# Where an opened matmul group is closed: at the end of a filler step, or at the start of the next one

## The chip, the cores and the metric

The kernel runs on all 8 cores of one Trainium2 chip. Each core works alone on its share: one of four batches and one half (8 heads, 512 columns) of the 1024 features. No data passes between cores. The metric is device time in microseconds (us) of the slowest core.

## The reference

With x of shape (4, 4096, 1024):

```python
xn = layernorm(x)
q, k, v = split(xn @ qkv_weights)          # 16 heads of 64, causal softmax attention
s  = softmax(mask(q @ k / 8)) @ v
xq = clip(round(xn / x_scale), -128, 127)  # x_scale = max|xn| / 127 per row
g  = silu((xq @ weight_q.T) * x_scale * weight_scale + bias)
out = x + s * g
```

(k is reshaped without the usual transpose, which is why the kernel scatters it in an unusual order; this doesn't matter here.)

## The kernel before

One Python program, `build_program`, appends instructions to five lists, one per engine, in the order in which its helpers are called. Every engine then replays its list strictly in that order. So the order of calls in the program is the order of work on each engine, and a wait of one instruction holds up all that stand behind it on the same engine.

**Phase 1** (up to about 600 us) walks over the 32 row tiles of x. For each it normalises, transposes and projects k (`emit_tile_a1`), and in between it pours in the steps that make v, the gate g and q of the first four chunks of 512 rows (`pump_merged`). The diff leaves this phase alone.

**Phase 2** is attention, by chunks c = 0 to 7 of 512 query rows (`emit_attention_chunk`). A chunk has four head pairs P, and each pair 4c+4 key blocks jb. One (P, jb) is a *unit*. In a unit the program emits, in this order: a piece of the gating of the pair before, if one is due (`pend_gate`, one of ga1, ga2, gb1, gb2, at jb 0, 2, 3 and 4, ahead of which it calls `close_open()`); the two matmuls Oa and Ob of the unit three back (L794, L798); the two score matmuls into sT (L735, L741; in the diagonal blocks L748 to L773); the exp on ScalarE (L780); and then a call of `pump()`. sT has two buffers and eT three.

`pump()` is the filler. Phase 2 still has to prepare the chunks 4 to 7, and `pump()` spreads that work over the units, usually one step of it per unit (`budget` is 1 in all units here that have steps left). The steps of a chunk stand in two lists: `flatA` (28 small steps of layernorm, quantisation and transposes, one that ends them, then v, then the gate), and `ib["lst"]` (q), which is taken up as soon as the 29th step of `flatA` is done.

The steps that matter here are the matmul groups, 12 per chunk: four q groups (`emit_qkv_f`, L538), four v groups (`emit_v_sub`, L555) and four gate groups (`emit_ffn_oc`, L585). Each group is 8 matmuls of 512 columns that accumulate in the one PSUM tile `pm`. It is cut into two steps of 4 matmuls each. The first half carries the tag "open": `pm` is then half summed, and nothing else may write it until the second half has run. The second half also emits what empties `pm`: ScalarE copies it to qT (L544) for q, VectorE copies it to v_aug (L562) for v, and VectorE multiplies it into g1s (L590) for the gate. The gate then has a chain of its own: t_b on GpSimd (L594), tanh on ScalarE (L600), gT on VectorE (L605), and the next g1s stands behind that gT in VectorE's list. The first matmul of any group waits until `pm` has been emptied of the group before it (`dep["pm_free"]`). `pm` has other users too: the single-row product of `emit_ffn_pre` (L569) and the eight tiny matmuls of ga2 (L848, L852).

`drain_open()` runs the second half wherever the last step taken was an open one. Before the change, `pump()` calls it after its step, so both halves of a group are emitted one behind the other.

Of the 52 groups in phase 2, four (q of chunk 3) are emitted in attention chunk 1, and 12 each in the attention chunks 2 to 5. The place of each is (pump number within the chunk, and the gating piece that stands at the start of that unit, if any):

- chunk 1: q at 1 (ga1), 2, 3 (ga2), 4 (gb1)
- chunk 2: q at 30 to 33; v at 35, 36, 37 (ga1), 38; gate at 41 (gb2), 42, 43, 44
- chunk 3: q at 30, 31, 32, 33 (ga1); v at 35 (ga2), 36 (gb1), 37 (gb2), 38; gate at 41 to 44
- chunk 4: q at 30 to 33; v at 35 to 38; gate at 41 (ga1), 42, 43 (ga2), 44 (gb1)
- chunk 5: q at 30 to 33; v at 35 to 38; gate at 41 to 44

The pumps 34 and 39 of a chunk carry steps without any instruction, pump 40 carries `emit_ffn_pre`. In chunk 2 pump 39 has ga2 ahead of it.

Of the kernel before, what the change touches and what calls it, by code (L numbers as in the profile page):

```python
# [67 lines left out]
def build_program(S=4096):  # L68
# [600 lines left out]
    def a_substeps(tc):  # L669
# [31 lines left out]
        return steps, stepsB  # L701

    def emit_attention_chunk(c, pump, close_open, drain_pre, drain_full):
        for P in range(NPAIR):
            if P == 1:
                drain_full()
# [10 lines left out]
            for jb in range(njb):  # L717
                if P == 0 and jb == 4 * c - 1:
                    drain_pre()
# [85 lines left out]
                pend_av.append(mk_av())  # L805
                att["unit"] += 1
                pump()
            while pend_av:
                pend_av.pop(0)()
# [154 lines left out]
    def append_tc(tc):  # L964
        sa, sb = a_substeps(tc)
        sa = norm(sa)
        for j, (fn, tag) in enumerate(sa):
            if tag and tag.startswith("tilesdone"):
                qa_tiles_end[tc] = len(flatA) + j + 1
                sa[j] = (fn, None)  # L970
            elif tag and tag.startswith("vdone"):
                qa_pre_end[tc] = len(flatA) + j + 1
                sa[j] = (fn, None)
        flatA.extend(sa)
        qa_end[tc] = len(flatA)
        qb[tc] = norm(sb)
# [25 lines left out]
    def stepA():  # L1002
        fn, tag = flatA[ia["k"]]
        fn()
        ia["k"] += 1
        return tag

    def stepB():
        fn, tag = ib["lst"][ib["k"]]
        fn()  # L1010
        ib["k"] += 1
        return tag

    def drain_open():
        while (ia["k"] > 0 and ia["k"] < len(flatA)
               and flatA[ia["k"] - 1][1] == "open"):
            stepA()
        while (ib["k"] > 0 and ib["k"] < len(ib["lst"])
               and ib["lst"][ib["k"] - 1][1] == "open"):
            stepB()  # L1020

    for c in range(NTC):
        def drain_pre(c=c):
            while ia["k"] < qa_pre_end.get(c, qa_end.get(c, 0)):
                stepA()

        def drain_full(c=c):
            while ia["k"] < qa_end.get(c, 0):
                stepA()
        while ia["k"] < qa_start.get(c, 0):  # L1030
            stepA()
        if c == 0:
            drain_pre()
        while ib["k"] < len(ib["lst"]):
            stepB()
        if NMERGE <= c + 2 < NTC:
            append_tc(c + 2)
        ib["lst"] = qb.get(c + 2, [])
        ib["k"] = 0
        ib["gate"] = qa_tiles_end.get(c + 2, 0)  # L1040

        uc = {"u": 0}
        nunits = NPAIR * (4 * c + 4)
        dlA = 0

        def pump():
            uc["u"] += 1
            left = max(1, nunits - uc["u"] + 1)
            needed = max(0, dlA - ia["k"]) + (len(ib["lst"]) - ib["k"] + 1) // 2
            budget = max(1, -(-needed // left))  # L1050
            for _ in range(budget):
                if ib["k"] < len(ib["lst"]) and ia["k"] >= ib["gate"]:
                    stepB()
                elif ia["k"] < len(flatA):
                    stepA()
                else:
                    break
            drain_open()

        def close_open():  # L1060
            drain_open()
        emit_attention_chunk(c, pump, close_open, drain_pre, drain_full)
    while ia["k"] < len(flatA):
        stepA()
# [36 lines left out]
def _get_nc(S):  # L1101
    if S not in _NC_CACHE:
        _NC_CACHE[S] = build_program(S)
    return _NC_CACHE[S]
# [44 lines left out]
```

How the kernel before makes its waits and increments, by code:

```python
    def replay(self, eng, handle, sems):  # L47
        seen = {}
        own = self.OWN.get(eng)
        prior = 0
        for waits, fn, inc in self.ops[eng]:
            allw = list(waits)
            if own is not None and prior > 0:
                allw.append((own, prior))
            for s, v in allw:
                if seen.get(s, 0) >= v:
                    continue
                handle.wait_ge(sems[s], v)
                seen[s] = v
            ins = fn(handle)
            if inc is not None:
                s, amt = inc
                ins.then_inc(sems[s], amt)
                if s == own:
                    prior += amt
```

## Time and profile before

| | us |
|---|---|
| median of the runs | 1527.43 (1524.6 to 1530.26) |
| the profiled execution | 1525.28 |
| its slowest core's span (core 4) | 1523.7 |
| spans of all eight cores | 1503.6 to 1523.7 |
| matmuls busy (PE), core 4 | 1067.1 |
| ScalarE busy (ACT), core 4 | 720.1 |
| VectorE busy (DVE), core 4 | 575.8 |

In the rows further down, PE is TensorE with its matmuls, ACT is ScalarE, DVE is VectorE and POOL is GpSimd. A row of the timeline gives the start and the length in us, the engine, the line, what is written from what, and how many instructions are merged into the row; in brackets stands the idle time of the engine before it and whose end released it. A matmul's listed length holds the pipe's tail, so the pace of back-to-back matmuls is read from start to start. PEclk is the share of full TensorE clock that was granted in a stretch: 1.00 is 2.4 GHz and 0.50 would be 1.2 GHz throughout.

### The profile page before, as it was taken

The page shows a single profiled execution, that of the slowest core. Times are in us where ns is not written, and L with a number is a line of the kernel's source. Part 1 is how long each engine was busy: PE and PEld are TensorE (multiplying, and loading weights), DVE is VectorE, ACT ScalarE, POOL GpSimd, SP SyncE. Part 2 cuts the span into 40 slices and gives each one's busy share as a digit, 9 for nine tenths or more (in the row PEclk, how much of TensorE's full clock was granted, in tenths as well). Part 3 has the DMA queues.
Part 4 walks back from the last instruction along what each step waited for, and adds up shares of the span by engine and source line. Part 5 has one row for each costly group of instructions (what it writes and reads, how often), then busy time and mean ns, then how long its engine had stood idle before and what let it go on. Part 6 is the DMA issues. An engine that isn't in the chain of part 4 may idle for free.

```text
span 1523.7 us, 17831 instructions; the slowest of 8 cores (1503.6 to 1523.7 us)
## 1 busy us (share of the span) xinstructions
PE 1067.1 (70%) x5163; PEld 435.6 (29%) x5200; DVE 575.8 (38%) x1086; ACT 720.1 (47%) x905; POOL 302.1 (20%) x412
## 2 busy tenths in 40 slices
PE   0235545545455556987888888888888888888886
PEld 0112221212222122543333333433333333323232
DVE  0385283483553554337437335431822111111111
ACT  0121131220211112475445456548646888888886
POOL 1341250430513543113122013011301000000000
PEclk9956856758666655698887998989888999899999
DMA  7110010000000121112111002001100000000000
GB/s 115 49 42 14 14 42 0 28 29 0 29 27 28 56 70 49 42 42 70 43 29 56 15 15 84 8 8 42 36 8 21 14 15 14 15 28 9 11 17 14
DMA packets 24463, 47.46 MB, mean 31 GB/s; under 512 B 4272, under 2 KB 7472, under 8 KB 24368
## 3 DMA queue, kind: packets, MB, share of 16 engines
q1 hardware_dynamic: 15552, 25.34, 5.7%
q0 software_dynamic: 8816, 20.98, 5.6%
q8 instruction: 44, 0.72, 0.2%
q14 instruction: 51, 0.42, 0.1%
HBM read 40.54 MB, written 8.39 MB: 32 GB/s over the span
## 4 chain that ended last, share of the span: by engine, by line
PE 35%; DVE 25%; ACT 18%; issue 9%; POOL 6%; DMA 6%; DVEq 1%; ACTq 0%; POOLq 0%; SPq 0%
ACT eT L780 16%; PE Oa L794 5%; PE pm L555 4%; PE pm L538 4%; PE Ob L798 4%; DMA xst<-x 3%; PE pm L585 3%; PE sT L735 3%; DVE t_r L433 3%; DVE t_b L437 3%; DMA w8n<-w 2%; DVE bnst L240 2%; PE pm L848 2%; DVE t_g L430 2%; PE pm L852 2%
## 5 line engine op out<-in xcount | busy, mean ns | idle before, releaser
L780 ACT ACTIVATE eT<-sT 128x1024 bf16<-128x1024 f32 (+1 forms) x576 | 549.5, 954 | 214.4 <-PE sT L741 121.4
L794 PE MATMUL Oa<-eT,v_aug 128*65 128x512 bf16 (+1 forms) x576 | 238.5, 415 | 2.8
L798 PE MATMUL Ob<-eT,v_aug 128*65 128x512 bf16 (+1 forms) x576 | 226.3, 397 | 0.0
L735 PE MATMUL sT<-qT,kTa 64*128 64x512 bf16 x448 | 182.2, 416 | 36.2 <-ACT eT L780 34.5
L741 PE MATMUL sT<-qT,kTa 64*128 64x512 bf16 x448 | 185.0, 422 | 0.0
L897 POOL DMA_DIRECT2D out<-outs x32 | 24.3, 760 | 687.5 <-DVE outs L890 602.4
L833 DVE TENSOR_TENSOR wpr<-Oa,gT 64x512 bf16<-64x512 f32 x32 | 21.8, 683 | 336.8 <-PE Ob L798 335.8
L301 PE MATMUL sT<-Wqk,xnK 128*128 128x512 bf16 x244 | 107.2, 614 | 51.2 <-ACT xnK L289 40.1
L735 PEld LDWEIGHTS sT<-qT,kTa 64*128 64x128 bf16 x448 | 40.3, 94 | 222.6 <-issue 219.9
L794 PEld LDWEIGHTS Oa<-eT,v_aug 128*65 128x65 bf16 x576 | 67.2, 117 | 106.0 <-issue 94.1
L585 PE MATMUL pm<-xnq,wqT 128*128 128x512 bf16 x251 | 75.0, 451 | 26.4 <-DVE g1s L590 20.4
L555 PE MATMUL pm<-Wv,xnq 128*128 128x512 bf16 x247 | 70.0, 430 | 24.4 <-DVE v_aug L562 18.8
L281 PE MATMUL pt<-idb_s,xnbf 128*128 128x128 bf16 x128 | 17.2, 280 | 95.8 <-POOL xqbf L269 83.1
L594 POOL TENSOR_SCALAR t_b<-g1s,wscb,biab 128x512 f32<-128x512 f32 x32 | 24.6, 769 | 296.1 <-DVE g1s L590 296.1
L289 ACT ACTIVATE xnK<-pt 128x1024 bf16<-128x1024 bf16 x32 | 32.8, 1025 | 98.8 <-PE pt L281 92.4
L305 ACT ACTIVATE ktmp<-sT 128x512 bf16<-128x512 f32 x32 | 19.1, 598 | 123.8 <-PE sT L301 123.8
L240 DVE BATCH_NORM_STATS2 bnst<-xst 128x6 f32<-128x512 f32 x64 | 44.4, 694 | 87.5 <-DMA xst<-x 82.0
L848 PE MATMUL pm<-idf_s,rows 1*128 1x1 f32 x256 | 50.5, 264 | 33.1 <-DVE wpr L837 21.8
L538 PE MATMUL pm<-xnq,Wqk 128*128 128x512 bf16 x246 | 60.8, 387 | 17.8 <-ACT qT L544 8.7
L798 PEld LDWEIGHTS Ob<-eT,v_aug 128*65 128x65 bf16 x576 | 69.5, 121 | 7.0 <-issue 0.5
L600 ACT ACTIVATE g1s<-t_b 128x512 f32<-128x512 f32 x32 | 20.2, 631 | 96.5 <-POOL t_b L594 96.5
L562 DVE CAST v_aug<-pm 128x512 bf16<-128x512 f32 x32 | 22.2, 694 | 113.4 <-PE pm L555 113.2
(122 smaller groups left out, 1603.1 us busy)
## 6 DMA issues: line engine op xcount, KB each, us to landing
xst<-x SPq DMA_DIRECT2D x96, 256.0 KB, 2.9
xres<-xr POOLq DMA_DIRECT2D x32, 256.0 KB, 3.7
out<-outs POOLq DMA_DIRECT2D x32, 256.0 KB, 2.8
Wqk<-wq POOLq DMA_DIRECT2D x1, 1024.0 KB, 14.8
Wqk<-wk POOLq DMA_DIRECT2D x1, 1024.0 KB, 25.8
Wv<-wv POOLq DMA_DIRECT2D x1, 1024.0 KB, 30.4
w8n<-w POOLq DMA_DIRECT2D x4, 256.0 KB, 2.7
wscb<-wsc SPq DMA_DIRECT2D x4, 0.5 KB, 6.7
```

The costliest lines, as they stand in the source:

```text
L240: sc.emit("vector", lambda v, buf=buf, h2=h2, bnst=bnst: v.bn_stats(bnst[:, 6 * h2:6 * h2 + 6], xst[:, 512 * buf:512 * buf + 512]), waits= ...
L301: c_mm = sc.emit("tensor", lambda t, kk=kk, xK=xK, slotA=slotA: t.matmul(slotA, xK[:, kk, :], Wqk[:, kk, 512:1024], start=(kk == 0), stop= ...
L433: v.scalar_tensor_tensor(t_r[:], txn[:, off:off + 512], inv, t_g[:], ALU.mult, ALU.subtract), inc="dv")
L538: c_mm = sc.emit("tensor", lambda t, kk=kk, f=f: t.matmul(pm[:], Wqk[:, kk, 128 * f:128 * f + 128], xnq[:, kk, :], start=(kk == 0), stop=( ...
L555: c_mm = sc.emit("tensor", lambda t, kk=kk, vs=vs: t.matmul(pm[:], xnq[:, kk, 128 * vs:128 * vs + 128], Wv[:, kk, :], start=(kk == 0), sto ...
L585: c_mm = sc.emit("tensor", lambda t, kk=kk, oc=oc: t.matmul(pm[:], wqT[:, kk, 128 * oc:128 * oc + 128], xnq[:, 8 + kk, :], start=(kk == 0) ...
L735: t.matmul(sT[par][:, o:o + w], kTa[0:64, P, 128 * jb:128 * jb + 128], qT[P][0:64, qb + o:qb + o + w], start=True, stop=True), waits=w0)
L741: qb=qb: t.matmul(sT[par][:, 512 + o:512 + o + w], kTa[64:128, P, 128 * jb:128 * jb + 128], qT[P][64:128, qb + o:qb + o + w], start=True, ...
L780: s.activation(eT[pe3][:].rearrange("p (b n) -> p b n", b=2)[:, :, o:o + w], sT[par][:].rearrange("p (b n) -> p b n", b=2)[:, :, o:o + w], ...
L794: sc.emit("tensor", lambda t: t.matmul(Oa[:, o:o + w], v_aug[:, jb, 65 * hA:65 * hA + 65], eT[pe3][:, o:o + w], start=(jb == 0), stop=(jb ...
L798: c_av = sc.emit("tensor", lambda t: t.matmul(Ob[:, o:o + w], v_aug[:, jb, 65 * hB:65 * hB + 65], eT[pe3][:, 512 + o:512 + o + w], start=( ...
L848: c_lt = sc.emit("tensor", lambda t, it=it: t.matmul(pm[0:128, 2 * it:2 * it + 1], rows[64:65, 128 * it:128 * it + 128], idf[64:65, 64:65] ...
```

## The change

`pump()` calls `drain_open()` ahead of its budget of steps and no longer behind it. A group whose first half was emitted in one unit gets its second half at the next call of `pump()`, or at the next `close_open()` if a gating piece comes first. In between stand the Oa, Ob and score matmuls of the next unit. So that no step of another list, and no other user of `pm`, comes between the halves, `drain_open()` is also called at the start of `drain_pre`, of `drain_full` and of each chunk.

```diff
     for c in range(NTC):
         def drain_pre(c=c):
+            drain_open()
             while ia["k"] < qa_pre_end.get(c, qa_end.get(c, 0)):
                 stepA()
 
         def drain_full(c=c):
+            drain_open()
             while ia["k"] < qa_end.get(c, 0):
                 stepA()
+        drain_open()
         while ia["k"] < qa_start.get(c, 0):
             stepA()
...
             budget = max(1, -(-needed // left))
+            drain_open()
             for _ in range(budget):
                 if ib["k"] < len(ib["lst"]) and ia["k"] >= ib["gate"]:
                     stepB()
@@
                     stepA()
                 else:
                     break
-            drain_open()
```

No instruction is added, removed or changed in shape; only the places of some instructions in the engines' lists change.

## Rows read from the trace of the kernel before

**Rows 1.** The page, part 1: engine, busy us, share, instructions.

```profile
PE 1067.1 (70%) x5163; PEld 435.6 (29%) x5200; DVE 575.8 (38%) x1086; ACT 720.1 (47%) x905; POOL 302.1 (20%) x412
```

**Rows 2.** Timeline, units without filler in chunk 6, ScalarE, then TensorE.

```profile
1174.00 8.84 ACT L780 ACTIVATE eT<-sT 128x1024 bf16<-128x1024 f32 x8
...
1173.21 0.39 PE L735 MATMUL sT<-qT,kTa 64*128 64x512 bf16 x1
...
1174.08 0.39 PE L735 MATMUL sT<-qT,kTa 64*128 64x512 bf16 x1
```

**Rows 3.** Timeline, v groups of chunk 5, TensorE, with the unit between two groups.

```profile
1127.48 0.39 PE L735 MATMUL sT<-qT,kTa 64*128 64x512 bf16 x1
1127.48 0.39 PE L741 MATMUL sT<-qT,kTa 64*128 64x512 bf16 x1
1128.03 1.67 PE L555 MATMUL pm<-Wv,xnq 128*128 128x512 bf16 x7 [0.16 <-issue]
1129.54 0.38 PE L794 MATMUL Oa<-eT,v_aug 128*65 128x512 bf16 x1
1129.75 0.38 PE L798 MATMUL Ob<-eT,v_aug 128*65 128x512 bf16 x1
1130.07 0.39 PE L735 MATMUL sT<-qT,kTa 64*128 64x512 bf16 x1
1130.07 0.39 PE L741 MATMUL sT<-qT,kTa 64*128 64x512 bf16 x1
1130.71 1.89 PE L555 MATMUL pm<-Wv,xnq 128*128 128x512 bf16 x8 [0.26 <-DVE v_aug L562]
1132.44 0.38 PE L794 MATMUL Oa<-eT,v_aug 128*65 128x512 bf16 x1
...
1133.62 1.89 PE L555 MATMUL pm<-Wv,xnq 128*128 128x512 bf16 x8 [0.26 <-DVE v_aug L562]
```

**Rows 4.** Timeline, the same stretch, VectorE.

```profile
1129.88 0.69 DVE L562 CAST v_aug<-pm 128x512 bf16<-128x512 f32 x1 [14.23 <-PE pm L555]
```

**Rows 5.** Timeline, phase 1, TensorE: groups with nothing between them.

```profile
247.51 1.89 PE L555 MATMUL pm<-Wv,xnq 128*128 128x512 bf16 x8 [1.01 <-DVE v_aug L562]
250.42 1.89 PE L555 MATMUL pm<-Wv,xnq 128*128 128x512 bf16 x8 [1.01 <-DVE v_aug L562]
...
262.79 3.57 PE L585 MATMUL pm<-xnq,wqT 128*128 128x512 bf16 x8 [1.01 <-DVE g1s L590]
267.38 3.57 PE L585 MATMUL pm<-xnq,wqT 128*128 128x512 bf16 x8 [1.01 <-DVE g1s L590]
...
281.03 1.89 PE L538 MATMUL pm<-xnq,Wqk 128*128 128x512 bf16 x8 [0.90 <-ACT qT L544]
283.81 1.89 PE L538 MATMUL pm<-xnq,Wqk 128*128 128x512 bf16 x8 [0.90 <-ACT qT L544]
```

**Rows 6.** Timeline, q groups of chunk 5, TensorE, then ScalarE.

```profile
1118.57 1.89 PE L538 MATMUL pm<-xnq,Wqk 128*128 128x512 bf16 x8
...
1120.83 0.39 PE L735 MATMUL sT<-qT,kTa 64*128 64x512 bf16 x1
...
1121.46 1.89 PE L538 MATMUL pm<-xnq,Wqk 128*128 128x512 bf16 x8 [0.25 <-PE sT L741]
...
1124.35 1.89 PE L538 MATMUL pm<-xnq,Wqk 128*128 128x512 bf16 x8 [0.25 <-PE sT L741]
...
1120.61 0.60 ACT L544 ACTIVATE qT<-pm 128x512 bf16<-128x512 f32 x1 [1.00 <-PE pm L538]
1121.37 1.03 ACT L780 ACTIVATE eT<-sT 128x1024 bf16<-128x1024 f32 x1 [0.16 <-PE sT L741]
```

**Rows 7.** Timeline, gate groups, TensorE: four of chunk 5, two of chunk 4.

```profile
1142.51 1.67 PE L585 MATMUL pm<-xnq,wqT 128*128 128x512 bf16 x7 [0.55 <-ACT xscBs L574]
...
1145.19 1.89 PE L585 MATMUL pm<-xnq,wqT 128*128 128x512 bf16 x8 [0.26 <-DVE g1s L590]
...
1148.64 1.89 PE L585 MATMUL pm<-xnq,wqT 128*128 128x512 bf16 x8 [0.81 <-DVE g1s L590]
...
1152.15 1.89 PE L585 MATMUL pm<-xnq,wqT 128*128 128x512 bf16 x8 [0.87 <-DVE g1s L590]
...
1003.57 1.90 PE L585 MATMUL pm<-xnq,wqT 128*128 128x512 bf16 x8
1006.49 1.89 PE L585 MATMUL pm<-xnq,wqT 128*128 128x512 bf16 x8 [0.69 <-DVE g1s L590]
```

**Rows 8.** Busy time by stretch, with PEclk: phase 1 (three rows), then phase 2.

```profile
247.50:256.40 8.90, 5.79 (x24) 2.33 (x26) 2.08 (x3) 0.00 (x0) 0.00 (x0) 1.00 0.00 0
275.40:286.60 11.20, 7.49 (x31) 2.85 (x32) 2.77 (x4) 3.02 (x5) 1.47 (x2) 1.00 0.00 0
262.70:271.90 9.20, 7.15 (x16) 2.04 (x16) 2.77 (x4) 1.26 (x2) 1.54 (x2) 0.55 0.00 0
1128.00:1139.00 11.00, 10.19 (x47) 4.00 (x46) 2.50 (x4) 4.28 (x5) 0.00 (x0) 1.00 0.01 1
```

## The prediction

> **What bounds the kernel now.** I read the page first for the engines' loads, then the timeline engine by engine inside phase 2, since an average over the span can't say which engine sets the pace where the filler runs. By the page [rows 1] no engine is full; the answer lies in two kinds of stretch.
>
> In units without filler, ScalarE runs its exps without a break: eight in 8.84 us, 1.10 us each [rows 2]. TensorE alone, while it runs ahead of ScalarE's backlog, needs 0.87 us from one score matmul to the next (1174.08 - 1173.21). There ScalarE is the bound, by 0.23 us a unit. In units with a matmul group TensorE adds 8 matmuls, and ScalarE idles (its exp of 1.03 us and a copy of 0.60 us fit in a unit of 2.9 us with over a microsecond left) [rows 6]. There the TensorE list sets the pace, and what is lost on it is lost for the whole core: the next scores, and so the next exp, come that much later, and nothing later gives it back, because ScalarE then has no backlog.
>
> The row on which all hangs is the wait for `pm`. A v group starts 1130.71, the next 1133.62: 2.90 us apart [rows 3], of which the 8 matmuls take 1.73 (from its first to the start of Oa, 1130.71 to 1132.44) and the attention unit 0.87; the rest, about 0.3, is a wait for VectorE's copy. Now compare phase 1, where groups follow each other with nothing between: v groups again start 2.90 us apart (247.51, 250.42), with 1.01 us listed as idle before each [rows 5]. The two distances are equal. So emptying `pm` makes a fixed distance of 2.90 us between two v groups, and the attention unit costs nothing there: it runs inside the wait. The pieces of that wait: the last matmul of a group starts at about 1129.33 (0.21 before Oa), the copy starts at 1129.88 and takes 0.69 [rows 4], and the next group starts 0.14 after its end. From the last matmul's start to the next group's first: 0.55 + 0.69 + 0.14 = 1.38 us, where a matmul that doesn't wait would follow after 0.22. The wait is worth 1.16 us.
>
> **The change part by part.** No work is added. Between two scores of a series there are still 8 filler matmuls, but they are now the second half of group X and the first half of group Y, next to each other. The wait for the emptying of `pm` lies exactly between those two. The list on TensorE was: X first, X second, Oa, Ob, scores, Y. It becomes: X second, wait, Y first, Oa, Ob, scores, Y second. The attention unit that covered the wait now stands between the two halves of one group, where nothing waits. Behind the waiting first matmul of Y stand Oa, Ob and the next scores, and for those waits ScalarE.
>
> How many such places are there? Two groups in pumps that follow each other, with no gating piece at the start of the second's unit: with a gating piece, `close_open()` runs the second half of X ahead of it, the order on TensorE stays X, gating, unit, Y, and nothing changes. From the list of places: q has 1, 3, 2, 3 and 3 in the chunks 1 to 5, that is 12; v has 2, 1, 3 and 3 in the chunks 2 to 5, that is 9; the gate has 3, 3, 1 and 3, that is 10. Together 31 of 52 groups.
>
> *v, 9 places.* The distance becomes the bare one plus the unit that no longer hides: 2.90 + 0.87 = 3.77 against 2.90, +0.87 each [rows 2, 3, 5]. 9 x 0.87 = 7.8 us.
>
> *q, 12 places.* Bare distance 2.78 (281.03 to 283.81) [rows 5], now 2.89 [rows 6]. Lower bound 2.78 + 0.87 - 2.89 = +0.76. But the copy to qT now stands behind the exp of its unit in ScalarE's list. The exp starts 0.54 after its score matmul (1121.37 - 1120.83) and takes 1.03 [rows 6], so it ends 1.57 after it; the copy's 0.60 with 0.05 before it ends at 2.22; 0.14 later, at 2.36, the next first half starts; its four matmuls take 0.86 and Oa, Ob up to the next score matmul 0.53 (1129.54 to 1130.07) [rows 3]: a distance of 3.75, +0.86. An upper bound takes the 0.25 that TensorE stood still there before a group, now seen after a score matmul [rows 6], in place of 0.14: +0.97. I take the middle one, since both its ends are rows: 12 x 0.86 = 10.3 us (9.1 to 11.6).
>
> *Gate, 10 places.* Here the chain g1s, t_b, tanh, gT, g1s already holds the groups 3.45 to 3.51 us apart from the third on, and only the first distance is short, 2.68 [rows 7]. The new distance: from the start of g1s 0.69, 0.14 to the next first half, 0.86 for it, 0.87 for the unit, 0.65 from the first to the last matmul start of the second half, 0.55 to its g1s: 3.76. That is above 3.5, so the chain no longer decides and is hidden. A series of four: 3 x 3.76 - (2.68 + 3.45 + 3.51) = +1.6. Three series 4.9, the single place in chunk 4 (2.92 now) +0.8: 5.7 us. If the chain's slack counted fully against it, the lower bound would be 0.25 a place, 2.5 us.
>
> *The ends of the series.* The second half of the last v group moves into the unit after it, and `emit_ffn_pre` in the next finds `pm` not yet empty: its place comes 0.31 + 0.86 + 0.53 + 0.31 = 2.01 after the score matmul, `pm` is free at 0.31 + 0.65 + 1.38 = 2.34, +0.33 in three chunks (in chunk 2 ga2 lies there): +1.0. From q to v the same sum is 2.36 against 2.01, and 0.24 of it is lost there already (1127.48 to 1128.03, where 0.31 would do) [rows 3]: +0.1 each, +0.4. At the end of the four gate series half a group moves into a unit in which ScalarE's pace of 1.10 would have ruled over TensorE's 0.87 [rows 2]: -0.23 each, -0.9. Net +0.5.
>
> *The other edits.* The calls of `drain_open()` in `drain_pre`, `drain_full` and at the chunk's start find nothing open: the first two come where their loops have no step to run, and each series ended before the chunk did. Free. No DMA is moved: the steps that issue x loads (SP) or GpSimd work other than t_b are not open ones and stay in their unit. t_b moves with its group, and GpSimd is 20% busy [rows 1].
>
> Sum: 7.8 + 10.3 + 5.7 + 0.5 = 24.3 us on the profiled execution's 1525.3, which gives 1549.6. The median of the runs is 2.1 higher, so 1551.7; I say 1552. What isn't in the sum is the clock.
>
> **The rivals.**
>
> *A. The wait is there and the clock falls too.* A unit of 3.76 us has 8 filler matmuls and four of attention in it, TensorE streaming for 2.60 (1.73 + 0.87), 69%, where it was 90%. Against a fall: in phase 1, groups 2.90 and 2.78 us apart stream 60 to 62% of the time, and the clock stayed at 1.00 (2.4 GHz) [rows 8]. For it: gate groups in phase 1, 4.59 us apart, ran at a granted 0.55, close to 1.2 GHz, with 3.57 us a group in place of 1.89 [rows 5, 8], after a stretch of single-row products. A clock that is low when a series begins could stay low through it. Each unit at the low clock would add 3.57 - 1.89 = 1.68 for the group and about as much again in proportion, 0.7, for the attention matmuls: 2.4 us. If a third of the 31 units ran so: +25, 1577. If all did: +74, 1626.
> The Trainium skill, TensorE: Matmul & The Clock Gate, section "A second HAM failure mode: psum-queue depth-cycling", says that frequent small idles between matmul groups, caused by turning over PSUM, make the clock swing between its two levels. By that rule rival A would be the forecast. The trace only half agrees: two stretches with a 0.9 to 1.0 us idle before every group kept 1.00, the third didn't [rows 8].
>
> *B. The wait is covered after all.* If VectorE and ScalarE emptied `pm` fast enough, only the odd us would move, and the time would be 1525 to 1532. The 1.01 us idle before every back-to-back v group and the 0.90 before every q group in phase 1 speak against it [rows 5]: there both engines had nothing else to do and it was still paid.
>
> *C. Faster.* This would be the smoothing of load: half groups in a unit leave less TensorE time between two exps. Where a half group stood alone in a unit, the unit would take 1.73 and let ScalarE catch up. It decides only if TensorE's per-unit work falls below ScalarE's 1.10, and with a half group it is 1.73. Only the ends of the series gain, 0.23 each [rows 2]; even if all 13 series gave 0.23 and no wait appeared: -3, 1524. For over 2% it would need the clock: if phase 2 as a whole got a better clock through other timing, up to the 20 us by which the cores of one execution differ, 1507.
>
> **How the numbers follow.** Forecast 0.70, A 0.20, B 0.07, C 0.03. The likeliest: 1552, its own range 1544 (the lower bounds of q and gate: 24.3 - 1.2 - 3.2 = 20, less 3 for timing) to 1562 (q's upper bound and three or four units more at the low clock). The range over the cases that hold 8 in 10 is 1541 to 1576: below it lie B and C, above it the heavier half of A. A measurement of this kernel can tell about 2% (30 us) from no change. The forecast and the light end of A stay below 1558, the line for 2% slower; A mostly and the upper end of the forecast pass it. Faster 0.02, same 0.70, slower 0.28.
>
> **What would show it right or wrong.** In the timeline of chunk 5 after: rows of four matmuls at L555, a wait of about 1.0 us put down to v_aug L562, four more, Oa, Ob, scores; v groups 3.77 apart, q groups 3.75, gate groups 3.76. In the waits: idle before L538, L555 and L585 for `pm` up by about 25 us in all, busy times unchanged, PEclk in these series still 1.00. Everything after chunk 5 lies about 24 us later and is otherwise unchanged. Wrong would be: PEclk near 0.5 in the series (A); the same distances with no idle (B); or distances as I say but a span that grows by much less, which would mean that the lost time is given back in a place where I hold ScalarE to have no backlog.

## The result, and the profile after

The changed kernel takes 1551.6 us (median; before, in the same comparison, 1525.48). The ratio is 1.0161, with a 95% interval of 1.013 to 1.0192: slower by 25 us, which is clear of the noise and less than 2%. The forecast was 1552, from a median of 1527.4 before; in this comparison that median was 1525.5.

The waits of TensorE in the stretch where filler runs (600 to 1190 us of the changed kernel, core 4): who waited for whom, us in total, times, longest. First the three that the change makes:

```profile
PE pm L538 <- ACT qT L544: 14.8, 13, 2.0
PE pm L585 <- DVE g1s L590: 10.8, 11, 1.0
PE pm L555 <- DVE v_aug L562: 10.0, 10, 1.2
```

The same view of before, 600 to 1160 us:

```profile
PE pm L585 <- DVE g1s L590: 6.5, 10, 0.9
PE pm L555 <- DVE v_aug L562: 3.2, 7, 1.3
...
PE pm L538 <- ACT qT L544: 0.7, 1, 0.7
```

35.6 us in place of 10.4: 25 us more idle in front of groups. The busy times are as before (PE 1070.8 against 1067.1, ACT 718.7 against 720.1). The timeline of TensorE in chunk 5 after, v groups (start, length, engine, line, out<-in, count, idle before and its releaser):

```profile
1158.88 1.04 PE L555 MATMUL pm<-Wv,xnq 128*128 128x512 bf16 x4
1160.94 1.02 PE L555 MATMUL pm<-Wv,xnq 128*128 128x512 bf16 x4 [1.02 <-DVE v_aug L562]
1161.80 0.38 PE L794 MATMUL Oa<-eT,v_aug 128*65 128x512 bf16 x1
1162.01 0.38 PE L798 MATMUL Ob<-eT,v_aug 128*65 128x512 bf16 x1
1162.32 0.39 PE L735 MATMUL sT<-qT,kTa 64*128 64x512 bf16 x1
1162.33 0.39 PE L741 MATMUL sT<-qT,kTa 64*128 64x512 bf16 x1
1162.65 1.04 PE L555 MATMUL pm<-Wv,xnq 128*128 128x512 bf16 x4
```

The reader should see the four matmuls of one group's second half, a wait of 1.02 us, four of the next group's first half, and only then the attention unit. In [rows 3] the unit stood between the groups and 0.26 us of wait was left. The distance is 3.77 us (1162.65 - 1158.88).

The q groups of the same chunk, TensorE and then ScalarE; they answer to [rows 6]:

```profile
1143.21 0.39 PE L735 MATMUL sT<-qT,kTa 64*128 64x512 bf16 x1
...
1143.54 1.04 PE L538 MATMUL pm<-xnq,Wqk 128*128 128x512 bf16 x4
1145.73 1.02 PE L538 MATMUL pm<-xnq,Wqk 128*128 128x512 bf16 x4 [1.16 <-ACT qT L544]
...
1147.44 1.04 PE L538 MATMUL pm<-xnq,Wqk 128*128 128x512 bf16 x4
...
1143.76 1.02 ACT L780 ACTIVATE eT<-sT 128x1024 bf16<-128x1024 f32 x1 [2.08 <-PE sT L741]
1144.88 0.60 ACT L544 ACTIVATE qT<-pm 128x512 bf16<-128x512 f32 x1
```

The copy stands behind the exp. It ends at 1145.48, and TensorE goes on 0.25 later. The distance is 3.90.

The gate groups of chunk 5, which answer to [rows 7], 3.76 apart:

```profile
1172.15 1.04 PE L585 MATMUL pm<-xnq,wqT 128*128 128x512 bf16 x4
1174.20 1.02 PE L585 MATMUL pm<-xnq,wqT 128*128 128x512 bf16 x4 [1.01 <-DVE g1s L590]
...
1175.91 1.04 PE L585 MATMUL pm<-xnq,wqT 128*128 128x512 bf16 x4
```

Busy time by stretch for the three series, the columns as in [rows 8]; the last but two is the granted clock:

```profile
1138.00:1153.00 15.00, 11.40 (x51) 3.98 (x50) 0.00 (x0) 6.97 (x9) 0.30 (x1) 1.00 0.06 18
1154.00:1167.00 13.00, 9.96 (x46) 3.47 (x44) 2.08 (x3) 3.82 (x5) 0.00 (x0) 1.00 0.00 0
1171.00:1180.00 9.00, 6.97 (x33) 2.42 (x31) 2.24 (x4) 4.01 (x6) 1.53 (x2) 1.00 0.01 2
```

TensorE stays at 2.4 GHz through all three. Not every series runs at that level: in four of the 13 (q of chunk 1, v of chunks 2 and 3, the gate of chunk 4), and for part of the gate of chunk 2, the granted clock is partly 0.50, in both kernels. Summed over the 13 series, the time at 1.2 GHz is 17.6 us before and 17.5 after (mean of the eight cores, worked out from the granted clock between the exps at the ends of each series). So the clock has no part in the 25 us.

Where the time went by chunk, from one profiled execution of each kernel: the start of a chunk's first exp to that of the next chunk's, mean of the eight cores, after less before.

| | phase 1 | c0 | c1 | c2 | c3 | c4 | c5 | c6 | c7 |
|---|---|---|---|---|---|---|---|---|---|
| before, us | 593.0 | 33.9 | 56.4 | 109.2 | 127.0 | 140.7 | 155.3 | 136.0 | 164.0 |
| after less before | +1.9 | +0.4 | +2.3 | +5.6 | +4.7 | +5.5 | +6.7 | -0.8 | -1.3 |
| adjacent places | 0 | 0 | 1 | 8 | 6 | 7 | 9 | 0 | 0 |

The loss lies in the chunks that have adjacent groups. Phase 1 is the same code in both kernels, so its +1.9 shows by how much two executions differ anyway.

### The profile page after: what moved, and what is told of

Its sections match the earlier page's. It is cut to its first block, busy times and chain, and to the rows that moved or that the text cites. A ratio compares the mean times of both kernels' runs of the same rounds, so it can differ in the third digit from the quotient of the medians.

```text
span 1550.9 us, 17819 instructions; the slowest of 8 cores (1526.8 to 1550.9 us)
## 1 busy us (share of the span) xinstructions
PE 1070.8 (69%) x5161; PEld 435.1 (28%) x5200; DVE 575.8 (37%) x1086; ACT 718.7 (46%) x905; POOL 302.1 (19%) x412
## 4 chain that ended last, share of the span: by engine, by line
PE 36%; DVE 25%; ACT 18%; issue 9%; POOL 6%; DMA 5%; DVEq 1%; ACTq 0%; POOLq 0%; SPq 0%
ACT eT L780 16%; PE Oa L794 5%; PE pm L555 4%; PE pm L585 4%; PE Ob L798 4%; PE pm L538 3%; PE sT L735 3%; DVE t_r L433 3%; DVE t_b L437 3%; DMA xst<-x 3%; DMA w8n<-w 2%; PE pm L848 2%; DVE t_g L430 2%; PE pm L852 2%; DVE bnst L240 2%
## 5 line engine op out<-in xcount | busy, mean ns | idle before, releaser
L741 PE MATMUL sT<-qT,kTa 64*128 64x512 bf16 x448 | 183.3, 418 | 0.0
L897 POOL DMA_DIRECT2D out<-outs x32 | 24.3, 758 | 695.7 <-DVE outs L890 613.3
L555 PE MATMUL pm<-Wv,xnq 128*128 128x512 bf16 x247 | 72.6, 433 | 33.3 <-DVE v_aug L562 27.1
L562 DVE CAST v_aug<-pm 128x512 bf16<-128x512 f32 x32 | 22.2, 694 | 134.1 <-PE pm L555 133.9
```

What stands on the lines that cost most here:

```text
L555: c_mm = sc.emit("tensor", lambda t, kk=kk, vs=vs: t.matmul(pm[:], xnq[:, kk, 128 * vs:128 * vs + 128], Wv[:, kk, :], start=(kk == 0), sto ...
L741: qb=qb: t.matmul(sT[par][:, 512 + o:512 + o + w], kTa[64:128, P, 128 * jb:128 * jb + 128], qT[P][64:128, qb + o:qb + o + w], start=True, ...
```

## The experiments

The theory: a lost microsecond wherever the second half of one group and the first half of the next stand next to each other on TensorE, because emptying `pm` then lies bare. The rivals: that every split group costs something (1.61% over 52 groups), that the clock is lower, and that the order costs something through ScalarE.

**One kind of group at a time, and only where no other group follows.** The changed kernel, in which `pump()` still closes a group in its own unit unless a condition holds:

```diff
+            if not (ib["k"] > 0 and ib["k"] <= len(ib["lst"]) and ib["lst"][ib["k"] - 1][1] == "open"):
+                drain_open()
```

This is `q_only`: the condition says that the last step taken from the q list was an open half. It is written likewise for v, for the gate, and for the 21 groups behind which no other group stands in the next unit or a gating piece comes first (`free_only`).

> Only the q groups are left open over a unit; v and gate groups are closed in their own pump, as before. Adjacency theory (cost only where the second half of one group and the first half of the next stand next to each other, with the emptying of pm between them): 12 such places, each the distance after of 3.90 less 2.89 before = 1.0 us, and 0.3 at each of the four steps from q to v: +13 us, ratio 1.008 to 1.009. Split theory (every opened half costs the same, 25 us over 52 groups = 0.48): 20 q groups, +10 us at most, and it must agree with the cost per group of the other three runs. Clock theory (the loss is a lower TensorE clock in the series): PEclk under 1.00 in the q series, cost not tied to places.

> Only the v groups are left open over a unit. Adjacency theory: 9 places of 0.87 us and 0.33 at three steps to the single-row product: +9 us, ratio 1.006. Split theory: 16 groups, +7.7 us. Clock theory: no fixed relation to places.

> Only the gate groups are left open over a unit. Adjacency theory: the chain over GpSimd and ScalarE already held these groups 3.5 us apart, so 10 places give only +5.7, less 0.9 at the ends: +5 us, ratio 1.003. Split theory: 16 groups, +7.7 us. If the waits for pm simply added up without the chain's cover, 10 x 0.87 = +8.7.

> Groups are left open only where no other group follows in the next unit, or where a gating piece closes them first; the 31 adjacent places are closed in their own pump as before. Adjacency theory: 21 opened groups, none adjacent, only the ends of series move: within 2 us of before, ratio 1.000 +- 0.002. Split theory: 21 x 0.48 = +10 us, ratio 1.007.

| split groups | of them adjacent | ratio to before | 95% interval |
|---|---|---|---|
| 20 q | 12 | 1.0134 | 1.0101 to 1.0168 |
| 16 v | 9 | 1.0073 | 1.0045 to 1.0101 |
| 16 gate | 10 | 1.0026 | 1.0001 to 1.0051 |
| 21, none adjacent | 0 | 0.9996 | 0.9972 to 1.0019 |

The last row is the cleanest, but it holds fewer split groups than its label says. In nine of the 21, `close_open()` brings the second half right behind the first on TensorE; in the trace of `free_only` 12 groups really have other matmuls between their halves (in two of them only the last Oa and Ob of a pair, a case that the prediction took for no change), and in the changed kernel 31 + 12 = 43. By that count the split theory asks for 25/43 x 12 = 7 us, +0.5%. The interval ends at +0.2%: tearing a group apart costs nothing that could be measured, as long as no other group touches it. In the first row the waits of v and gate stay those of before, and that of q is the one of after:

```profile
PE pm L538 <- ACT qT L544: 14.7, 13, 1.9
PE pm L585 <- DVE g1s L590: 6.8, 11, 0.9
PE pm L555 <- DVE v_aug L562: 3.5, 8, 1.3
```

v came out near what was expected (+11 us against +9) and so did the gate (+4 against +5). q missed: +20 us against +13, with an interval that begins above the 1.008 to 1.009 expected. The three add up to 2.3%, more than the 1.6% of all together; with the widths of the intervals the two may just meet. The q series of chunk 3 explains a part: in the profiled execution it took 4.7 us more than before at only two adjacent places, with 3.1 us more at the low clock. Why the clock was low there stays open.

**Half a group per unit.** One bank; a pump that closes a group opens none:

```diff
+            k0 = ia["k"] + ib["k"]
             drain_open()
+            if ia["k"] + ib["k"] > k0:
+                budget -= 1
```

> One bank; a pump that closes a group takes no further step, so a unit holds one half group at most and each group takes two units. Adjacency theory: between the second half of a group and the first half of the next stands a whole unit, so no wait is paid that is not covered. Also units of 1.73 us in place of one of 2.60 + 0.3 and one without filler of 1.10, in which ScalarE is the bound: for 36 q and v groups 3.46 against 3.99 = -0.5 each, for 16 gate groups 3.5 against 4.6 = -1.1 each at most: -15 to -35 us, ratio 0.977 to 0.990. Rival (ScalarE's backlog makes smoothing worthless, only waits count): 21 x 0.3 and the gate's waits, -12 us at most, ratio 0.992. Split theory: slower than the changed kernel.

1.0048 (1.0017 to 1.0080): a miss of my own theory, which had asked for 0.977 to 0.990. The split theory missed as well (the run was faster than the changed kernel), and so did the rival that only waits count (0.992). By chunk, against before, it was -6.5, +17.1, -7.0 and +2.9 us in c2 to c5. So the series gain and something takes it back. Core 3 in chunk 3, TensorE and then ScalarE:

```profile
895.55 2.94 PE L585 MATMUL pm<-xnq,wqT 128*128 128x512 bf16 x8 [1.68 <-ACT xscBs L574]
899.50 0.55 PE L848 MATMUL pm<-idf_s,rows 1*128 1x1 f32 x2 [1.01 <-DVE g1s L590]
...
903.57 3.31 PE L585 MATMUL pm<-xnq,wqT 128*128 128x512 bf16 x8
...
895.50 1.02 ACT L780 ACTIVATE eT<-sT 128x1024 bf16<-128x1024 f32 x1
900.50 0.63 ACT L600 ACTIVATE g1s<-t_b 128x512 f32<-128x512 f32 x1 [3.98 <-POOL t_b L594]
903.74 1.02 ACT L780 ACTIVATE eT<-sT 128x1024 bf16<-128x1024 f32 x1 [2.60 <-PE sT L741]
```

The longer series now runs into units with gating pieces. There `close_open()` pushes the second half in front of the piece, and ga2, which uses `pm` too, waits for g1s. A whole group, the wait, and eight single-row products at the low clock stand between two scores: 8.2 us from one exp to the next. The mean of the eight cores for this unit is 7.6 us; before, when it held no group, it took 2.5.

**Two banks.** The groups use `pm` and the bank of `pt` in turn. This was run with the order of after (`two_banks`), with that of before (`two_banks_b`) and with half a group per unit (`half_two_banks`). Of the edit only the choice of the bank is shown:

```diff
+        if half == 0 and bk["on"]:
+            if bk["key"] == "pm_free":
+                bk["t"], bk["key"] = pt[:].bitcast(F32), "pt_free"
+            else:
+                bk["t"], bk["key"] = pm[:], "pm_free"
```

> The changed kernel's order, but in phase 2 the groups accumulate in turn in pm and in the bank of pt (read as 512 f32), so a group waits for the emptying of the group two before it. Adjacency theory (the wait for the single bank is the whole cost): the 1.0 us waits before q and v groups vanish, v and q distances fall to about 2.6 us, the gate stays at 3.5 by its own chain: 24 to 30 us less than the changed kernel, and 3 to 7 us less than before: ratio to before 0.995 to 0.998. Rival (the order itself costs, through ScalarE's late exps or the weights): it stays near 1.016.

> The same two banks with the order of before (both halves of a group together). Adjacency theory: before, the attention unit covers 0.87 of the 1.16 us wait and 0.3 is left; without it 21 v and q places save 0.3 each, and the gate nothing: 6 us less than before, ratio 0.996, and equal to the run with the changed order within 3 us.

> One half group per unit, and two banks. Adjacency theory: with a unit between groups nothing waits for a bank, so the second bank brings nothing more: the same as one half per unit with one bank, within 3 us.

1.0047 (1.0016 to 1.0077), 1.0031 (1.0009 to 1.0053) and 0.9960 (0.9939 to 0.9981). With the second bank the changed order costs 0.2% more than the old one, where with one bank it cost 1.6%. The waits of the groups for the copies to qT and v_aug and for g1s are gone from the list of waits. That shows the wait for the single bank to be nearly the whole difference between the two orders. The expectations of the times failed in all three runs, though. Neither order became faster than before. A part of the reason comes out below: a group that starts right behind gb2 waits for the bank of `pt`. `two_banks_b` has two such groups that land there, the gate group at pump 41 of chunk 2 and the v group at pump 37 of chunk 3; with the unit behind it, each place took 2.8 and 3.3 us longer than before (mean of the eight cores). That is 6 of the 11 us between the +5 measured and the -6 expected; the rest stays open. And half a group per unit did gain from the second bank, 0.9% or 13 us, where I had written that nothing waits. The unit between two groups covers only 0.87 of the 1.16 us, as [rows 3] had shown already; 0.3 us in each of some 36 distances makes an estimated 10 us of it.

**Half a group per unit, away from the gating pieces.** From chunk 2 on, no group is opened in a unit whose next one is among a pair's first five (jb 0 to 4, where the gating pieces stand), nor a gate group in a pair's last three units; what is left over slips into the next chunk. Of the edit only the rule is shown:

```diff
+                    if tag == "open" and (nx < 5 or (      # nx: jb of the next unit
+                            gate_step and nx > 4 * c + 4 - 3)):
+                        break
```

> The same with the single bank pm. A unit covers 0.87 of the 1.16 us wait, so 0.3 is left in each of some 36 distances between groups: 10 us more than with two banks, ratio 0.987 to 0.994. If the bank doesn't matter once the halves stand alone, it equals the run with two banks.

> One half group per unit, two banks, and no group is opened in a unit whose next unit begins with a gating piece (nor a gate group in the last three units of a pair), so no half is pushed together with a gating piece; the steps left over slip into the next chunk. Collision theory (one half per unit loses its gain where its series meets the gating pieces: +18 us and +15 us behind the series of chunks 3 and 5): those losses vanish and what the series gain stays, 0.5 us for a q or v group and up to 1.1 for a gate group, 8 us a chunk in four chunks: -20 to -30 us against before, ratio 0.980 to 0.987. Rival (the loss belongs to spreading itself, that is, to a lower clock and ScalarE's backlog in longer series): ratio 0.996 as without the rule, or worse, since the series are still longer.

> The same with two banks, but chunk 2, which has only 48 units for 57 steps, keeps the order of before (whole groups), so nothing slips out of it. Collision theory: -8 us in each of the chunks 3 to 5 and nothing in chunk 2: -15 to -25 us, ratio 0.984 to 0.990. If it beats the run with the rule in all chunks, chunk 2 is too short for spreading.

With one bank: 0.9901 (0.9868 to 0.9934), 1506.1 us, faster than both kernels and within what was expected of it. The rule does two things at once, though: it keeps the groups away from the gating pieces, and it moves steps into the units of later chunks. No run separates the two. That half a group per unit lost its gain to the collisions is therefore argued from the rows above, not shown by itself. With two banks the rule gained nothing, where 0.980 to 0.987 had been expected: 1.0008 (0.9988 to 1.0029), and with chunk 2 left in the old order 1.0013 (0.9996 to 1.0029, expected 0.984 to 0.990). The timeline of the first of these two says why. TensorE in chunk 4, core 5, then VectorE:

```profile
916.44 0.60 PE L754 MATMUL sT<-qT,kTa 64*128 64x512 bf16 x1
919.11 1.86 PE L567 MATMUL pt<-Wv,xnq 128*128 128x512 bf16 x4 [2.06 <-DVE outs L903]
...
915.97 0.28 DVE L897 SCALAR_TENSOR_TENSOR outs<-pt,linvT,xres 128x64 f32<-128x64 bf16 x1 [2.55 <-PE pt L889]
...
918.68 0.28 DVE L903 SCALAR_TENSOR_TENSOR outs<-pt,linvT,xres 128x64 f32<-128x64 bf16 x1
```

(This kernel has more lines: L567 is the v group, L555 elsewhere, and L754, L897 and L903 are L741, L884 and L890.) The bank of `pt` isn't free. gb2 has just put its transposes there, and VectorE reads them in eight steps over 3 us; the rule lets a group start right behind gb2, and it landed in `pt`. Six such units stand in the chunks 3 to 5; they took 5.3 to 5.7 us each, and 1.8 to 2.6 in the run with one bank (mean of the eight cores). The last run changes that one thing: a group always takes `pm` if the next unit is among a pair's first seven. By the rule those are the groups that start in the unit of gb2 and in the one behind it.

```diff
-            if bk["key"] == "pm_free":
+            if bk["key"] == "pm_free" and not bk["late"]:      # late: nx < 7
```

> As the run with the rule and two banks, but a group that starts in the first seven units of a pair always takes pm. Theory (the second bank costs what it does because the group opened right behind the gating piece gb2 lands in pt, whose transposes VectorE is then reading in eight steps into outs: TensorE waits 2.1 to 2.4 us, unit periods of 5.3 to 5.7 us in place of about 2): those units return to about 2 us, 5 or more places of 2.2 us on a core, and a lower clock behind each of them goes too: ratio 0.985 to 0.992, at least as good as the one-bank run at 0.990. Rival (without the idle before the groups TensorE draws the lower clock anyway, 0.806 against 0.818 in the mean): ratio stays at 0.998 or above, with the 5.5 us units gone and the mean clock still at 0.806.

0.9844 (0.9801 to 0.9888): 1500.2 us, 23 us faster than before and, by the two ratios, some 48 faster than the changed kernel. The six units took 1.7 to 2.4 us each; that is 20 of the some 24 us between `skip_two_banks` and this run. The same place, core 4, where the group's first half (one of its four records is missing) starts while VectorE still reads `pt` (until 904.38):

```profile
901.86 0.39 PE L754 MATMUL sT<-qT,kTa 64*128 64x512 bf16 x1
902.40 0.81 PE L567 MATMUL pm<-Wv,xnq 128*128 128x512 bf16 x3 [0.16 <-issue]
...
904.10 0.28 DVE L903 SCALAR_TENSOR_TENSOR outs<-pt,linvT,xres 128x64 f32<-128x64 bf16 x1
```

The mean granted clock of the eight cores in the profiled execution went from 0.807 back to 0.821, and before's was 0.822; over the runs that the ratios compare the means are 0.806, 0.817 and 0.821. So the lower clock went with the waits behind gb2: without them it was nearly back, and the rival, that it would stay at 0.806, failed.

## Why the prediction was right, point by point

*The step that carried it* was comparing the distance of v groups with and without an attention unit between them, 2.90 and 2.90 [rows 3, 5], and concluding that the unit's 0.87 us had been free and would be paid. It was paid: 3.77 measured, 3.77 forecast.

*The count of 31 places* held: 25 us more idle in the waits, the loss only in the chunks that have such places, and none at all in the run that leaves the 21 others open. That a gating piece keeps the halves together holds in nine of its eleven places only; the two others cost nothing measurable.

*q* was mis-sized. The term was 12 x 0.86 = 10.3 us for a distance of 3.75; the place shown above has 3.90 (the other two of that series 3.94 and 3.89), +1.01 a place, which for all 12 would make 12.1. From the copy's end to TensorE's next matmul it took 0.25 us (1145.48 to 1145.73); the last section says why. I had taken the 0.14 seen behind VectorE's copy [rows 3, 4] and kept the 0.25, which stood in [rows 6], as the upper bound. The copy also began 0.10 after the exp's end, not 0.05. The row of the same kind of group was the better one.

*The gate* was mis-sized the other way. The distances are as forecast, 3.76. But the sum was to be +5.7, less 0.9 at the ends, that is 4.8; in the profiled execution of the changed kernel the four series, from the exp of the first gate unit to the fifth behind it, took 2.9 us more (mean of the eight cores), and 3.7 in that of the run with the gate alone. That run's +4 us (0.2 to 7.8) is too coarse to tell this from 4.8. What the sum had missed stands in ScalarE's timeline of before:

```profile
1142.24 1.02 ACT L780 ACTIVATE eT<-sT 128x1024 bf16<-128x1024 f32 x1
1146.20 0.63 ACT L600 ACTIVATE g1s<-t_b 128x512 f32<-128x512 f32 x1 [2.94 <-POOL t_b L594]
1146.92 1.02 ACT L780 ACTIVATE eT<-sT 128x1024 bf16<-128x1024 f32 x1
```

The tanh of the first gate group stood on ScalarE's list ahead of the next unit's exp and held it until 1146.92, 4.68 us after the one before, though its scores had been ready since 1144.9. After the change the second half, and the tanh with it, is emitted one unit later. In the changed kernel:

```profile
1170.58 1.02 ACT L780 ACTIVATE eT<-sT 128x1024 bf16<-128x1024 f32 x1 [0.28 <-PE sT L741]
1172.38 1.02 ACT L780 ACTIVATE eT<-sT 128x1024 bf16<-128x1024 f32 x1 [0.77 <-PE sT L741]
1175.21 0.63 ACT L600 ACTIVATE g1s<-t_b 128x512 f32<-128x512 f32 x1 [1.81 <-POOL t_b L594]
```

Those exps are 1.80 us apart. So ScalarE's list was a part of the path in the gate series, and I had followed TensorE's alone.

*The total was closer than its parts*, which is luck. Counted from exp to exp in the same way, the q and v series with the ends between them took 22.2 us more, where their terms make 19.5; the gate took 2.9, where its terms make 4.8. The errors of +2.7 and -1.9 us nearly cancel. That the time itself came out within 0.4 us is luck too, since the median before had moved by 2 us; the change was forecast as 24.3 us and measured, by the ratio, as 24.6 (19.8 to 29.3).

*Rival A* (the clock falls) didn't happen: the granted clock was 1.00 in the three series of chunk 5, and the time at 1.2 GHz over all 13 series was the same in both kernels. By the Trainium skill, TensorE: Matmul & The Clock Gate, section "A second HAM failure mode: psum-queue depth-cycling", small idles between groups that turn over PSUM make the clock swing. The trace doesn't agree: in the series of chunk 5, with 1.0 us idle in every 3.8, it stayed at 1.00.

*Rival B* (the wait is covered anyway) is refuted by the list of waits. *Rival C* (smoothing makes it faster) was priced at 3 us at most with adjacent halves, and rightly so for this change. But it named halves that stand alone in their units, and gave them no gain because 1.73 is above ScalarE's 1.10. The versions that are really faster are built so: with the rule about the gating pieces, and steps slipping into later chunks, they bring 1.0% with one bank and 1.6% with two.

## What to carry to other kernels

When work between two matmul groups looks like a cost, compare the groups' distance with a place where nothing lies between them: if both distances are equal, that work hides the emptying of the accumulator, and moving it away costs its full length. Splitting a group to spread it cost nothing measurable here, but what is emitted behind the split must not be the next group on the same bank. When filler is spread over more units, look at which units it reaches: here half a group per unit gained in its series and lost it again around the pieces that share a bank with it. And before counting on a second bank, look at who else uses it: here each group that was to start while the bank was still being read cost some 3 us.

## What the runs showed of the hardware that I had not expected

A wait that has long been met seems still to cost time when it stands behind the one that ends last. In the series of chunk 5 a q group starts 0.25 us after ScalarE's copy has ended (1145.48 to 1145.73), but the first one that waits starts after 0.15 (1141.08 + 0.60 to 1141.83):

```profile
1141.83 1.02 PE L538 MATMUL pm<-xnq,Wqk 128*128 128x512 bf16 x4 [1.19 <-ACT qT L544]
...
1141.08 0.60 ACT L544 ACTIVATE qT<-pm 128x512 bf16<-128x512 f32 x1 [0.23 <-ACT eT L780]
```

In phase 1 it is 0.14 for every q group (the copy at 280.29 for 0.60, the next group at 281.03), and behind VectorE's copy it is 0.14 or 0.15 in both phases (1129.88 + 0.69 to 1130.71).

The difference lies in the program. The first matmul of a q group lists, behind the wait for `pm_free`, one for the scores that last read its part of qT (`att_q_free`, semaphore `pe`). `replay` leaves a wait out if one for the same or a higher value has been issued before, so the second wait is issued for some groups only: in the attention chunks 4 and 5 for the third and fourth, in chunk 3 for the fourth, in the chunks 1 and 2 for all, in phase 1 for none. Over the eight cores of the changed kernel, where the copy came last, the start followed after 0.25 or 0.26 us in all 76 places with the second wait and after 0.14 in all 32 without. So the 0.11 us go with that wait, though it had long been met. No run takes it out, and it stands in both kernels.
